# The normalised rows of two layer norms, transposed in DVE blocks and SBUF transfers instead of on TensorE

## What is computed

```
x = x + xattn(layernorm(x), ctx, mask)          # 64 queries, 512 keys
x = x + attn(layernorm(x))                      # q, k, v with bias; 64 tokens per sequence
h = relu(layernorm(x) @ ternary(W1).T + b1)     # 512 -> 2048
x = x + h @ ternary(W2).T + b2                  # 2048 -> 512
ternary(W) = clip(round(W / (mean(abs(W)) + 1e-5)), -1, 1)
```

## Time and profile before

| | us |
|---|---|
| three runs | 1743.09, 1744.25, 1746.99 |
| median | 1744.25 |
| the profiled execution | span 1745.7; no time of its own is given |
| cross-attention, with its hand-over | 0 to 784 |
| self-attention loop | 784 to 1225 |
| hand-over into the feed-forward | 1225 to 1266 |
| feed-forward loop | 1266 to 1745.7 |

### The profile page before, as it was taken

The page is one execution under the profiler, slowest core; times in us unless marked ns, Lnnn a source line. Parts: engine busy times, 40 slices in busy tenths (PEclk is TensorE's granted clock), DMA queues, the critical chain, the costliest instruction groups (busy, mean ns, idle before and its releaser), DMA issues.

```text
span 1745.7 us, 38877 instructions
## 1 busy us (share of the span) xinstructions
PE 1689.3 (97%) x16268; PEld 1416.7 (81%) x16268; DVE 1032.7 (59%) x1492; ACT 701.8 (40%) x1689; POOL 216.0 (12%) x300
## 2 busy tenths in 40 slices
PE   6899999999999999998999999999899999999999
PEld 4688878788878788787888898989688888888887
DVE  3655556555565555667677777776674445544543
ACT  2555555665555566566422222323222222222221
POOL 1000000000000000122111121211032012202200
PEclk9999999999999999999999999999999999999999
DMA  6011111111111111333010101001101101100000
GB/s 218 13 62 62 62 62 61 52 59 62 61 62 55 48 54 54 132 132 139 26 49 24 48 24 41 31 27 57 51 31 49 49 1 49 48 17 31 25 24 24
DMA packets 48668, 95.00 MB, mean 54 GB/s; under 512 B 5792, under 2 KB 14112, under 8 KB 47264
## 3 DMA queue, kind: packets, MB, share of 16 engines
q1 hardware_dynamic: 48544, 93.16, 15.7%
HBM read 67.97 MB, written 25.17 MB: 53 GB/s over the span
## 4 chain that ended last, share of the span: by engine, by line
PE 90%; DVE 6%; issue 2%; ACT 2%; DMA 0%; DVEq 0%; SPq 0%; ACTq 0%
PE project L339 49%; PE project L1273 13%; PE scores L685 4%; PE scores L1791 3%; PE probs_t_psum L1791 3%; PE scores L1789 3%; PE probs_t_psum L1789 3%; PE probs_t_psum L694 3%; PE attended_t L711 2%; PE probs_t_psum L1379 2%; PE scores L491 1%; PE attended_t L1398 1%; DVE ff_weight_scratch L1224 1%; PE attended_t L1252 1%; DVE w_ternary L1227 1%
## 5 line engine op out<-in xcount | busy, mean ns | idle before, releaser
L1273 PE MATMUL project<-ff_xt,w_ternary 128*128 128x512 f32 x1024 | 256.4, 393 | 0.0
L1273 PEld LDWEIGHTS project<-ff_xt,w_ternary 128*128 128x128 f32 x1024 | 190.0, 188 | 38.4
L1282 ACT ACTIVATE hidden<-project,b_sb 128x512 f32<-128x512 f32 x128 | 88.2, 689 | 326.1 <-PE project L1273 326.1
L887 ACT ACTIVATE cross_scores_probs<-cross_scores_probs,exp_bias,logit_scale 128x128 f32<-128x128 f32 x256 | 122.6, 482 | 97.9 <-DVE exp_bias L1033 97.9
L339 PE MATMUL project<-self_xt_hi,self_w_hi 128*128 128x256 f32 x512 | 148.4, 290 | 3.2 <-DVE self_xt_lo L502 2.3
L339 PE MATMUL project<-self_xt_lo,self_w_hi 128*128 128x256 f32 x512 | 145.1, 283 | 0.0
L339 PE MATMUL project<-self_xt_hi,self_w_lo 128*128 128x256 f32 x512 | 145.0, 283 | 0.0
L887 ACT ACTIVATE cross_probs<-cross_scores,exp_bias,logit_scale 128x128 f32<-128x128 f32 x256 | 122.8, 483 | 0.4 <-DVE exp_bias L1033 0.4
L339 PE MATMUL project<-ctx_hi,cross_w_hi 128*128 128x512 f32 x256 | 107.0, 418 | 15.2 <-DVE ctx_lo L1052 15.2
L339 PE MATMUL project<-cross_w_hi,ctx_hi 128*128 128x512 f32 x256 | 108.8, 425 | 0.0
L339 PEld LDWEIGHTS project<-self_xt_hi,self_w_hi 128*128 128x128 f32 x512 | 98.4, 192 | 6.3 <-DVE self_xt_lo L502 2.6
(11 more groups left out here) (175 smaller groups left out, 4098.5 us busy)
## 6 DMA issues: line engine op xcount, KB each, us to landing
ctx_raw<-in_ctx SPq DMA_DIRECT2D x64, 256.0 KB, 4.0
cross_xt_raw<-in_x_t SPq DMA_DIRECT2D x64, 128.0 KB, 2.2
cross_x<-in_x SPq DMA_DIRECT2D x32, 256.0 KB, 3.0
x<-cross_x SPq DMA_DIRECT2D x32, 256.0 KB, 2.0
self_x<-x SPq DMA_DIRECT2D x32, 256.0 KB, 2.8
ff_w_raw<-in_w SPq DMA_DIRECT2D x2, 4096.0 KB, 13.8
x<-self_residual SPq DMA_DIRECT2D x32, 256.0 KB, 2.0
ff_x<-x SPq DMA_DIRECT2D x32, 256.0 KB, 3.4
```

Of the source, the lines that this page charges most:

```text
L887: last = nc.scalar.activation(c_p[buf][:, cols], c_s[buf][:, cols], ACT.Exp, bias=exp_bias[:, buf, g:g + 1], scale=logit_scale[:, parity(u ...
L1273: last = nc.tensor.matmul(PJ[m % 2][:], w1_q[:, c, cols], x_t[parity(v)][:, c, :], start=(c == 0 and x_t is fxt_hi), stop=(c == DC - 1 and ...
L1282: nc.scalar.activation(h_raw[:, m % 2, :], PJ[m % 2][:], ACT.Relu, bias=b1_sb[:, m:m + 1]).then_inc(h_relu, 1)
```

## The change

- For two normalised tiles together, DVE transposes blocks of 32x32 values inside SBUF (`ln_blocks`, one instruction of 128x1024). Each block stays in its group of 32 partitions.
- SP then moves the blocks to the right partitions by four SBUF to SBUF transfers (`ln_gather`, 128 KB each, from 32 partitions to all 128), back into `self_x_norm` or `ff_x_norm`. Channel 4k+j of a chunk's order ends at partition 4k+j, and the host puts the rows of W_q, W_k, W_v and W1 in the same order (`interleaved`).
- One ACT copy of 1024 values makes the high part and one DVE subtraction of 1024 the low part, both reading SBUF chunk by chunk. The matmuls read 256 (self) and 512 (feed-forward) consecutive values per chunk.
- PE's transposes of x leave, and with them X0 and X1 in the list of banks. Q0 of a self unit and hidden(0) of a feed-forward unit wait for the low parts.
- Tensors in SBUF are placed anew, and the region for descriptors that are made on the chip is set to 1024 bytes.

```diff
+def ln_blocks(xn, blocks):
+    return nc.vector.transpose(
+        blocks.rearrange("p (j i r) -> p i j r", j=4, r=32),
+        xn.rearrange("p t (c j k) -> p (t c) j k", j=4, k=32))
+def ln_gather(e, xn, blocks, done):
+    whole = xn.rearrange("p t (a n) -> p t a n", a=4)
+    for a in range(4):
+        e.dma_start(whole[:, :, a, :], blocks[32 * a:32 * a + 32, :]).then_inc(done, 16)
+sx_chunks = sxn[:].rearrange("p t (a c r) -> p c (t a) r", a=4, r=32)
+def self_x_hi(e, v):
+    wait(e, G.ln_in, total(v, 64, 64))
+    nc.scalar.activation(sxt_hi[:], sx_chunks, ACT.Copy).then_inc(G.xt_hi, 1)
+def self_x_lo(e, v):
+    wait(e, G.xt_hi, total(v, 1, 1))
+    nc.vector.tensor_tensor(sxt_lo[:], sx_chunks, sxt_hi[:].bitcast(F32), ALU.subtract) \
+        .then_inc(G.xt_lo, 1)
...
-s_full_uses = ["Q0", "Q1", "K0", "K1", "V0", "V1", "X0", "O0", "X1", "O1"]
-SB = Banks(["Y1", "O1"], s_full_uses,
+s_full_uses = ["Q0", "Q1", "K0", "K1", "V0", "V1", "O0", "O1"]
+SB = Banks(["O1"], s_full_uses,
... self_sync, step
+if kind == "full":
+    self_ln_gather(e, later(u, 2))
... self_pe
+if name == "Q0":
+    wait(e, G.xt_lo, total(later(u, 1), 1, 1))
... self_act, full step
+    full(u, "V1")
+    self_x_hi(e, v)
... self_dve, full step
     self_ln_normalise(e, w)
+    self_ln_transpose(e, w)
 maxima(u, 1)
...
-    x_lo(u, w, 0)
+    self_x_lo(e, w)
...
 a_lo(u, 1)
-    x_lo(u, w, 1)
... cross_sync, last step
+self_ln_gather(e, S_SECOND)
 load_self_x(e, Unit(1, 0))
... cross_dve, last step
 self_ln_normalise(e, S_SECOND)
+self_ln_transpose(e, S_SECOND)
 maxima(u, 3)
... ff_act
-if more and m in (3, 5, 7, 9):
+if more and m in (5, 10):
+    ff_x_hi(e, v, m // 5 - 1)
... ff_dve
-if m in (2, 4, 6, 8):
-    ff_ln_normalise(e, v, (m - 2) // 2)
+if m in (2, 3, 6, 7):
+    ff_ln_normalise(e, v, (0, 1, 2, 3)[(2, 3, 6, 7).index(m)])
+if m in (3, 7):
+    ff_ln_transpose(e, v, m // 4)
+if m in (5, 10):
+    ff_x_lo(e, v, m // 5 - 1)
```

More of the change, by code:

```diff
@@ L439, in self_ln_normalise @@
         def self_ln_normalise(e, v):
+            wait(e, G.xt_lo, total(v, 1))
             for t in range(NT):
@@ L463, in build, with self_ln_transpose, self_ln_gather @@
         SLOT = [(pair % 2) * 4 + pair // 2 for pair in range(PAIRS)]
[L465 to L469, removed]
+        sx_chunks = sxn[:].rearrange("p t (a c r) -> p c (t a) r", a=4, r=32)
+        tokens_of = lambda xt, c, first, n: (xt[:, c].rearrange("p a r -> p (a r)")
+                                             [:, first:first + n])
+        def self_ln_transpose(e, v):
+            wait(e, G.xn, total(v, NT, NT))
+            wait(e, G.ln_in, total(v, 64))
+            ln_blocks(sxn[:], s_ln_t[:]).then_inc(G.ln_t, 1)
+        def self_ln_gather(e, v):
+            wait(e, G.ln_t, total(v, 1, 1))
+            ln_gather(e, sxn[:], s_ln_t, G.ln_in)
         def self_qk_products(e, bank, n, w, before_last=None):
@@ L736, in self_qk @@
                 if n == 0 and w == 1:
-                    for t in range(NT):
-                        b, before = K.banks.at(u, f"x{t}", "last")
-                        e.wait_ge(C.pj_free[b], before + 1)
+                    e.wait_ge(G.xt_lo, 1)
                 self_qk_products(e, bank, n, w).then_inc(C.pj_full[bank], 1)
@@ L939, in step @@
                 queries_out(u, 1)
+                if not ahead:
+                    self_x_hi(e, S_FIRST)
                 a_hi(u, K.nt - 1)
             def last_step(u):
-                for t in range(NT):
-                    bank = full(u, f"x{t}", "last")
-                    self_x_hi(bank, t).then_inc(G.xt_hi, 1)
                 exponentials(u, 0)
@@ L960, in last_step @@
                 probs_t_out(u, 3)
[L961 to L964, removed]
+                full(u, "v1", "last")
+                self_x_hi(e, S_SECOND)
                 a_hi(u, K.nt - 1)
@@ L1107, in last_step @@
             def last_step(u):
-                self_ln_normalise(e, S_FIRST)
                 maxima(u, 0)
                 residual(later(u, -1), K.nt - 1, "last_but_one")
-                for t in range(NT):
-                    bank = full(u, f"x{t}", "last")
-                    self_x_lo_out(bank, t, t + 1, C.pj_free[bank])
                 maxima(u, 1)
@@ L1431, in last_step @@
                 v_proj(u, 1, "last")
+                transposes(u, 0)
+                attend_waits(u, 0)
+                attend(u, 0)
+                o_proj(u, 0, "last")
+                transposes(u, 1)
+                e.wait_ge(fxt_lo_ready, 2)
                 for name in ("V0", "V1"):
@@ L1590, in full @@
                 return bank
-            def x_lo(u, v, t):
-                bank = full(u, f"X{t}")
-                wait(e, G.xt_hi, total(v, NT, t + 1))
-                self_x_lo(bank, t).then_inc(G.pj_free[bank], 1)
             def a_hi(u):
@@ L1750, in step @@
                             .then_inc(fx_in[parity(w)], 16)
+                if kind != "last":
+                    for n in range(2):
+                        ff_ln_gather(e, later(u, 1), n)
                 for t in range(FT):
```

245 lines of the change are left out of this document (102 added, 143 removed).

## The result

| | before | after |
|---|---|---|
| runs | 4 | 4 |
| median, us | 1745.18 | 1778.84 |
| lowest to highest | 1743.09 to 1746.99 | 1775.56 to 1780.65 |
| ratio, 95% interval | | 1.0194, 1.018 to 1.0207 |
| span of the profiled execution | 1745.7 | 1777.4 |

What follows compares the result with a forecast made beforehand. The prediction took TensorE (busy 97%) as the bound, with DVE ending last at places. Terms -12.9 + 6.5 - 0.9 + 6.5 + 6.2 = +5.4 gave 1749.6 against the median, stated as 1749.5 us; range 1736 to 1760.

Steps and rivals of the forecast that it cites:

- feed-forward loop: Feed-forward loop: 28 removed groups of four PE transposes save 0.46 us each, added DVE work costs nothing: -12.9 us.
- self loop, 12 units: Self loop, ternary-weight units: longer DVE row behind V1 makes at_lo and O1 0.54 us later per unit: +6.5 us.
- cross to self, units 0 and 1: Hand-over from cross-attention: later Q0 +4.0 and low clock +2.5, in all +6.5; units 0 and 1 save 0.9.
- self to feed-forward: Last self unit into feed-forward: V1 7.6 later, hidden(0) 5.2 later, plus 1.0 for a possible clock drop: +6.2 us.
- the bank of K1 and p_norm their slack: Self units: the block transpose delays K's and V's copies and p_norm, but slack of 1.5 us at both hides it.
- One pass: Self units on DVE: a block transpose costs one pass over 1024 values, 1.22 us, hidden; two would be 2.4.
- the price of x_lo: Self units on DVE: the 1024-wide low part of x takes 1.225 us instead of 0.69.
- The low clock behind the idle: Cross-to-self hand-over: after PE idles some 5 us, a stretch at the 1.2 GHz level costs +2.5; bounds 0 and 2.5.
- The rule against 128x128 transposes on DVE: Skill's advice for TensorE; taken strictly, removed groups gain nothing, sum +19.2, about 1762; the prediction kept the rows' sum.

Runs made afterwards that it cites:

- after_shift108: The changed kernel with 54 more transposes (108 instructions) on PE in a never-run branch ahead of the self loop; 1754.6 us, ratio 1.005 to the kernel before.
- before_shift40: The kernel before, without the change, with 20 transposes (40 instructions) added in the branch that does not run; 1749.12 us, ratio 1.002.

## Why the prediction was wrong

By its terms, from the milestones above, with after_shift108 as the change without the code's place:

| term | forecast | measured |
|---|---|---|
| feed-forward loop | -12.9 | -14.2 |
| self loop, 12 units | +6.5 | +8.7 (after_shift108) |
| cross to self, units 0 and 1 | +5.6 | +3.8 (after), +6.8 (after_shift108) |
| self to feed-forward | +6.2 | +6.5 (after), +6.8 (after_shift108) |
| code fetched again | no term | +26.9 in the loop (35.6 - 8.7), +24.2 by the medians |

- **The step that failed** is the one called "Self loop, 12 units with ternary weights: +6.5". It priced the removed transposes as time on PE and the added work as time on DVE, and took it that PE's instructions are always at hand. The transposes taken out ahead of the loop (107 instructions with their waits) also moved the code, and the loop came to lie across eight blocks: +24.2 us that no term held. No rival held that either; they all share the assumption. Views that would have raised the question were at hand: the q8 line of the page, and its packets, of which none came at the returns of the self loop. They show that the loop stayed loaded; by how little, before_shift40 shows.
- **Feed-forward loop.** Right in mechanism, 1.3 too small. From the third on, the blocks of eight matmuls start 3.62 or 3.63 us apart throughout:

```profile
1414.30 1.98 PE L1282 MATMUL project<-ff_xt,w_ternary 128*128 128x512 f32 x8
...
1417.92 1.98 PE L1282 MATMUL project<-ff_xt,w_ternary 128*128 128x512 f32 x8
...
1421.55 1.98 PE L1282 MATMUL project<-ff_xt,w_ternary 128*128 128x512 f32 x8
```

- **Self loop without the fetch.** Right in place and mechanism, 2.2 too low. From residual(2,0) to residual(13,0) a unit took 337.80 / 11 = 30.71 us in after_shift108 and 329.08 / 11 = 29.92 before: 0.79 a unit, forecast 0.54. From residual(13,0) to residual(14,0) nothing was lost (24.08 and 24.10), so the 12 units cost 8.7. The row of DVE behind V1 gave 0.56 of it (907.00 to 912.03 for 1171.81 to 1176.28). The rest is K0's copy on ACT, late behind the block transpose: V0 needs its bank. Before, a copy ended at 1044.27 and V0 started at 1045.55; in after_shift108 V0 starts as the copy ends, and 0.15 to 0.2 later in its unit:

```profile
1055.70 0.82 ACT L538 ACTIVATE self_k_t<-project,bk_sb 128x256 f32<-128x256 f32 x2
...
1056.58 0.50 PE L347 MATMUL project<-self_w_hi,self_xt_hi 128*128 128x512 f32 x1
```

  The prediction gave the bank of K1 and p_norm their slack and did not look at K0's. One pass was right, and so was the price of x_lo (groups by line):

```profile
L427 DVE STREAM_TRANSPOSE self_blocks_t<-self_x_norm 128x1024 f32<-128x1024 f32 x16 | 19.9, 1245 | 1.7
L531 DVE TENSOR_TENSOR self_xt_lo<-self_x_norm,self_xt_hi 128x1024 fp32r<-128x1024 f32 x16 | 19.6, 1226 | 23.4 <-ACT self_xt_hi L527 23.4
```

- **Cross to self.** The sum was near, +5.6 for +3.8 or +6.8, but by luck. Q0 came 6.1 later, forecast 4.0; the gather took 5.8 from its first issue to ACT's start and not 4.5. SP's queue and ACT:

```profile
773.33 2.64 SPq L435 DMA_DIRECT2D self_x_norm<-self_blocks_t  x4
```

```profile
779.10 1.06 ACT L527 ACTIVATE self_xt_hi<-self_x_norm 128x1024 fp32r<-128x1024 f32 x1 [4.25 <-DMA self_x_norm<-self_blocks_t]
```

  Four issues took 2.64, not 4 x 0.43, and from the last issue's end to ACT's start it was 3.1. By the Trainium skill's rule (DMA: Bandwidth & Descriptors, Anatomy of one DMA) the estimate was 2.3 for one and 3.6 for all four; the trace has 2.9 in the median for one and 5.8 to the use of all four, so it differs. The low clock behind the idle came as forecast (781 to 785 above), but as a cost of 2.5 it did not: the kernel before had a low stretch there too, 0.56 in 787 to 794, which the term did not count, and by residual(2,0) the changed kernel was only 3.8 behind.
- **Self to feed-forward.** V1 came 7.9 later from residual(14,0) on (17.87 for 10.02), forecast 7.6; hidden(0) 6.5, forecast 5.2, and 6.2 with the clock.
- **The rule against 128x128 transposes on DVE.** The Trainium skill (VectorE: DVE Perf Modes, Rules for kernel authors) would have them on TensorE where PSUM will do. Here the version with all of them on DVE is the fastest that ran, 1721.29, and DVE had idle time where they were put. That does not refute the rule: the kernel before, with its transposes on TensorE, was not given the like reorderings.

## What to carry to other kernels

Removing instructions ahead of a loop moves the loop's code. Before a few us are summed up, look whether the engine's instruction queue is quiet during the loop, how many instructions a pass has and where it starts in its block of 256; a few runs with instructions in a branch that never runs show how much the place is worth. A chain that is read from the trace priced the other terms to 2.2 us or better, one of them by luck: three reorderings of DVE, ACT and SP, each aimed at a wait that the forecast had named, took 29.9 us off together (1754.6 to 1724.7).

## What the runs showed of the hardware

- Moving PE's code by 150 instructions that never run made an otherwise unchanged kernel 1.9% slower (1.0192, 1.0175 to 1.0209); by 220, not at all. The pattern repeats after 256.
- A return to a loop start that had to be fetched cost PE two stops, 1.9 and 2.7 us in the pass shown, and about 9 packets of 16 KB a pass. The granted clock fell to the 1.2 GHz level behind the stops: in the mean of 7 us it was 0.51 or 0.52 at three returns and 0.76 at two.
- A loop of 1692 or 1729 instructions across seven blocks of 256 was not fetched again. Across eight it was fetched in all passes where it reached 105 or more instructions into the eighth. Where it reached 33 into it, one trace has a fetch in two passes of five and another in all five, and the times differed from run to run.
- Four gathers of 128 KB in 512-byte pieces took 5.8 us from the first issue to their use, and SP needed 625 ns in the median for each issue, where an issue of a load of `self_x` took 360.
